# A fused RWKV-and-MoE layer: two value products in fp32r terms, and another order of the weight halves

## The chip, the cores and the metric

The kernel runs on one NeuronCore of a Trainium2 chip. The metric is device time in microseconds of one launch, as the median of several runs, lower is better. The engines named here: TensorE (PE, matrix products), VectorE (DVE), ScalarE (ACT, activation functions), GpSimd (POOL), SyncE (SP, which issues all DMA). Each engine runs its own list of instructions in order; semaphores hold one engine for another.

## The reference

Two layers over x of shape (8, 512, 512): batch, token, feature. The first is an RWKV time mix, the second a mixture of eight small experts with the top two chosen. Each has a residual and a layer norm behind it. Cut to what matters:

```python
shifted = jnp.pad(hidden, ((0, 0), (1, 0), (0, 0)))[:, :-1]
key   = hidden * time_mix_key   + shifted * (1.0 - time_mix_key)
value = hidden * time_mix_value + shifted * (1.0 - time_mix_value)
rec   = hidden * time_mix_receptance + shifted * (1.0 - time_mix_receptance)
k = key @ Wk
v = value @ Wv
r = jax.nn.sigmoid(rec @ Wr)
rwkv = _wkv(time_decay, time_first, k, v)   # a scan over the tokens: num, den, running max
x = _layernorm(x + (r * rwkv) @ Wo)
...
logits = x @ router_w.T ; gate = softmax(logits) * top2_mask
x = _layernorm(x + expert_mixture(x, gate))
```

## The kernel before

The features lie on the partitions. A **unit** is one batch and one block of 128 output features, so 8 batches of 4 units make 32 units, and the main loop runs over 32 **slots**, one unit each. All engines walk the same slots. A unit takes three products, key (PK), value (PV) and receptance (PR), each 128x512 out of four chunks of 128 input features; PE makes key(s+1), rec(s) and value(s+1) in slot s, and around them the projection of a token tile of the batch before (PP), its transposition (PT) and the expert layer (PH, PU).

The products are exact enough only if a plain fp32 operand is used, or if both operands are split. In the split form a value is written as high + low in the fp32r type (ACT copies the high half, POOL or DVE subtracts to get the low half), and each chunk gets three products: high by high, high of the input by low of the weight, low of the input by high of the weight. **Batch 0 uses the plain form** (`whole`, L316, weights as they were loaded into X1T, XN[0], XN[1]), **batches 1 to 7 the split form** (`split`, L330, L331, L336). The weight halves WKH, WKL, WVH, WVL, WRH, WRL are made during slots 0 to 6 while batch 0 is computed.

The order is written out by hand, engine by engine. What matters around the change:

- DVE in slot s: scan DEN (L871), times value (L878), scan NUM (L888), value now (L883), NU, the numerator (L895); then `scan_max` (L858) and `lead` (L864) of unit s+1, `gate` (L900) of unit s, `weigh` (L912, writes RW, the unit's result), and between them the mixes (L925) that make the inputs of the next batch: `mixes(b, which, chunks)`, with which 0 for key, 1 for value, 2 for receptance. In slot 1 DVE makes three key mixes of batch 1, then WKL's second half (L1048), then RW.
- ACT in slot s: two operations on PR (`receptance`), three Relu on PK (`decay_gates`), two more on PR (`log_g`, `factor`: without them `weigh` can't start), three Exp (`decay_exps`: without them the DEN scan can't start). All are recorded at L592. The high halves stand between them: WKH and WVH whole ahead of slot 0, WRH whole at the end of slot 0.
- POOL in slot s: DQ (L1213), wanted by `gate`; in slot 0 the four differences D of batch 1 (L1173), wanted by its mixes; in slot 1 the four blocks of WVL (L1244); then the low halves of batch 1's inputs (L1181).
- PE waits in `value(u)` for NU of unit u-1 (semaphore c), in `rec(u)` for RW of unit u-1 (rw), in `key(u)` for NUM of unit u-2 (num), and in batch 1's first unit for each high and low half of its input.

Of the kernel before, what the change touches and what calls it, by code (L numbers as in the profile page):

```python
# [29 lines left out]
def rwkv_moe_postln(nc, x, xt, vec, wk, wv, wr, wo, dr, up, tri, out):  # L30
    with ExitStack() as ctx:
# [169 lines left out]
        def sems(names):  # L201
            return {n: sem("s_" + n) for n in names.split()}

        q = sems("vec ws00 ws01 ws02 ws10 ws11 ws12 ws20 ws21 ws22 wo dr up tri out0 out1 out2 out3 xt0 xt1 xt2 xt3 xn0 xn1 xn2 xn3 xm0 xm1 xm2 xm3 "
# [104 lines left out]
        def _(eng):  # L309
            def whole(dst, stage, u, which):  # L310
                o = slice(128 * u, 128 * u + 128)
                eng.wait_ge(q[f"ws{which}{min(u, 2)}"], 16)
                for c in range(C):
                    if u == 0:
                        eng.wait_ge(q["kt"], C * which + c + 1)
                    last = eng.matmul(dst[:, :], stage[:, c, o], full(0, which, c), start=(c == 0), stop=(c == C - 1))  # L316
                return last

            def split(dst, weights, high, low, u, which, freed):
                b, j = divmod(u, C)  # L320
                o = slice(128 * j, 128 * j + 128)
                wh, wl = weights
                first = j == 0
                if b == 1:
                    eng.wait_ge(q["hw"], which + 1)
                    eng.wait_ge(q[("lwk", "lwv", "lwr")[which]], j + 1 if which else 2)
                for c in range(C):
                    if first:
                        eng.wait_ge(q["hi"], C * (3 * (b - 1) + which) + c + 1)
                    eng.matmul(dst[:, :], wh[:, c, o], high[:, c, :], start=(c == 0), stop=False)  # L330
                    eng.matmul(dst[:, :], wl[:, c, o], high[:, c, :], start=False, stop=False)  # L331
                    if first and C * (3 * (b - 1) + which) + c + 1 == ODD:
                        eng.wait_ge(q["rl1"], 1)
                    elif first:
                        eng.wait_ge(q["lo"], by_pool(C * (3 * (b - 1) + which) + c + 1))
                    last = eng.matmul(dst[:, :], wh[:, c, o], low[:, c, :], start=False, stop=(c == C - 1))  # L336
                    if j == C - 1 and c < C - 1:
                        last.then_inc(q[freed], 1)
                return last

            def key(u):
# [2 lines left out]
                last = split(PK[u % 2], (WKH, WKL), KH, KL, u, 0, "kc") if u >= C else whole(PK[u % 2], X1T, u, 0)  # L344
                last.then_inc(q["k"], 1)

            def value(u):
                eng.wait_ge(q["c"], u)
                last = split(PV, (WVH, WVL), VH, VL, u, 1, "vc") if u >= C else whole(PV, XN[0], u, 1)
                last.then_inc(q["v"], 1)  # L350

            def rec(u):
# [235 lines left out]
        def _(eng):  # L588
# [40 lines left out]
            def highs(b, which, chunks=range(C)):  # L629
                high, done, freed = ((KH, "k", "kc"), (VH, "v", "vc"), (RH, "r", "rc"))[which]  # L630
                for c in chunks:
                    eng.wait_ge(q["kt"], C * (3 * b + which) + c + 1)
                    if b > 1 and c < C - 1:
                        eng.wait_ge(q[freed], (C - 1) * (b - 2) + c + 1)
                    elif b > 1:
                        eng.wait_ge(q[done], C * b)
                    act("hi", high[:, c, :], full(b, which, c), ACT.Copy)
# [88 lines left out]
            eng.wait_ge(q["vec"], 16)  # L726
            act("etd", NTD, VEC[:, 0, :], ACT.Exp)

            def high_weights(i):
                stage, high = ((X1T, WKH), (XN[0], WVH), (XN[1], WRH))[i]  # L730
                for n in range(3):
                    eng.wait_ge(q[f"ws{i}{n}"], 16)
                act("hw", high[:, :, :], stage[:, :, :], ACT.Copy)

            decay_gates(0)
            decay_exps(0)
            high_weights(0)
            high_weights(1)
            for s in SLOTS:
                b, j = divmod(s, C)  # L740
                t2, t3 = NT * (b - 2), NT * (b - 3)
# [43 lines left out]
                if s < U - 1:  # L785
                    decay_exps(s + 1)
                if s == 0:
                    high_weights(2)
                if j == 3 and b and batch(b + 1):
                    highs(b + 1, 2, range(C - 1, C))  # L790
                for t in now[:1] if j == 3 and b < LAST else []:
# [61 lines left out]
        def _(eng):  # L853
# [190 lines left out]
                eng.tensor_tensor(D[:, c, :], XT[:, c, 1:T + 1], XT[:, c, 0:T], ALU.subtract).then_inc(q["d0"], 1)  # L1044

            def low_weights(lo):
                eng.wait_ge(q["hw"], 1)
                eng.tensor_tensor(WKL[:, lo:lo + 2, :], X1T[:, lo:lo + 2, :], WKH[:, lo:lo + 2, :].bitcast(F32),  # L1048
                                  ALU.subtract).then_inc(q["lwk"], 1)

# [9 lines left out]
            for s in SLOTS:  # L1060
                b, j = divmod(s, C)
                t2, t3 = NT * (b - 2), NT * (b - 3)
                now, past = tiles_of(s), tiles_of(s - 1)
                k = gated(s)
                scan_den(s)
                value_kept(s)
                if s == C:
                    eng.wait_ge(q["hi"], ODD)
                    eng.tensor_tensor(RL[:, C - 1, :], full(1, 2, C - 1), RH[:, C - 1, :].bitcast(F32), ALU.subtract)\
                       .then_inc(q["rl1"], 1)  # L1070
                scan_num(s)
                value_now(s)
                numerator(s)
                for t in past[1:]:
                    residual(t)
                if j == 0 and batch(b - 3):
                    residual2(t3 + 3)
                if j == 3 and s < U - 1 and batch(b - 2):
                    residual2(t2 + 1)
                if j == 1 and b:  # L1080
                    mixes(b + 1, 0, 3)
                if j == 3 and b:
                    mixes(b + 1, 2, 0)
                if j == 2 and s < U - 2 and batch(b - 2):
                    gated_low(b - 2)
                if C - 1 <= s < C * LAST:
                    gate(s)
                if s < U - 1:
                    scan_max(s + 1)
                    lead(s + 1)  # L1090
                if k is not None and s < U - 1:
                    gate_top(k)
                if s == 2:
                    mixes(1, 0, 3)
                if j == 3 and b:
                    mixes(b + 1, 2, 1)
                if not C - 1 <= s < C * LAST:
                    gate(s)
                if s == 1:
                    mixes(1, 0, 0, 1, 2)  # L1100
                if j == 2:
                    mixes(b + 1, 1, *(() if b else (0, 1)))
                if j == 3:
                    mixes(b + 1, 2, *((2, 3) if b else (0,)))
                if s == U - 1:
                    gate_scores(LAST - 1)
                if s < 2:
                    low_weights(2 * s)
                if s == C + 1:
                    eng.wait_ge(q["woh"], 1)  # L1110
                    eng.tensor_tensor(WOL[:, 2:4, :], X1T[:, 2:4, :], WOH[:, 2:4, :].bitcast(F32), ALU.subtract)\
                       .then_inc(q["wol1"], 1)
                weigh(s)
                for t in now[:1]:
                    residual(t)
                if j == 0 and b:
                    mixes(b + 1, 0, 0, 1, 2)
                if j == 2:
                    mixes(b + 1, 1, *(range(C) if b else (2, 3)))
                    if s < U - 2 and batch(b - 2):  # L1120
                        residual2(t2)
                if j == 3:
                    if b == 0:
                        mixes(b + 1, 2, 1, 2, 3)
                    if s < U - 1 and batch(b - 2):
                        residual2(t2 + 2)
                if s < U - 2 and gated(s + 1) is not None:
                    gate_scores(gated(s + 1))
# [34 lines left out]
        def _(eng):  # L1163
# [73 lines left out]
            difference(0, 2)  # L1237

            def low_weights(i, *blocks):
                stage, high, low, done = ((XN[0], WVH, WVL, "lwv"), (XN[1], WRH, WRL, "lwr"))[i - 1]  # L1240
                eng.wait_ge(q["hw"], i + 1)
                for j in blocks:
                    o = slice(128 * j, 128 * j + 128)
                    eng.tensor_tensor(low[:, :, o], stage[:, :, o], high[:, :, o].bitcast(F32), ALU.subtract)\  # L1244
                       .then_inc(q[done], 1)

            for s in SLOTS:
# [12 lines left out]
                if s == C + 1:  # L1260
                    eng.wait_ge(q["woh"], 1)
                    eng.tensor_tensor(WOL[:, 0:2, :], X1T[:, 0:2, :], WOH[:, 0:2, :].bitcast(F32), ALU.subtract)\
                       .then_inc(q["wol"], 1)
                if j == 0 and batch(b + 1):
                    for c in range(C):
                        difference(b + 1, c)
                if s == 1:
                    low_weights(1, *range(C))
                if j == 0 and batch(b - 3):
                    normalise2(t3 + 2)  # L1270
                if j == 2 and batch(b + 1):
# [82 lines left out]
```

## Time and profile before

| | us |
|---|---|
| median of 3 runs | 460.04 |
| lowest, highest | 459.71, 460.34 |
| the profiled execution | 459.98 |
| its span on the core | 458.2 |
| PE, busy in the span | 444.6 |
| DVE | 404.1 |
| ACT | 356.0 |
| POOL | 312.0 |

The span is what the trace covers; the time has 1.8 us more around it. Busy time is a sum over the whole span and says little of the first 66 us, in which the change lies: there the share of PE is lower and its waits have releasers, which the rows further down show. The granted TensorE clock stands at its full level in all of the forty slices but the last.

### The profile page before, as it was taken

To read this page: it belongs to the slowest core of one execution; us is meant where nothing else is said; L and a number is where in the kernel's file an instruction comes from. 1 tells how busy PE (TensorE), PEld (TensorE's weight loads), DVE (VectorE), ACT (ScalarE), POOL (GpSimd) and SP (SyncE) were. 2 spreads that over 40 slices of the span, in tenths; PEclk is the share of its full clock that TensorE was granted. 3 is DMA by queue.
4 is the path that set the end of the run, shared out by engine and by line. 5 is a ranking of instruction groups with operands and counts; after the bars stand their busy time and mean duration, and the time that the engine had idled before them with its cause. 6 is when DMAs were issued, how large, how long until landed. Compare 5 with 4: busy or idle time off the path is not lost.

```text
span 458.2 us, 6679 instructions
## 1 busy us (share of the span) xinstructions
PE 444.6 (97%) x1984; PEld 340.2 (74%) x1984; DVE 404.1 (88%) x616; ACT 356.0 (78%) x801; POOL 312.0 (68%) x300
## 2 busy tenths in 40 slices
PE   8999999999999999999999999999999999999993
PEld 3444567777888888888888888888888888888761
DVE  5989989899788989999898998989898996876976
ACT  1666757877888779888788888888798887768695
POOL 2355677588658998579858797569966694744334
PEclk9999999999999999999999999999999999999998
DMA  8703230033000042002320042100520022300016
GB/s 239 223 0 117 93 92 1 1 115 93 1 1 0 2 160 92 24 0 74 135 70 0 1 139 93 46 0 24 162 93 1 1 69 94 137 1 0 0 49 229
DMA packets 20244, 30.64 MB, mean 67 GB/s; under 512 B 2032, under 2 KB 7152, under 8 KB 20208
## 3 DMA queue, kind: packets, MB, share of 16 engines
q1 hardware_dynamic: 20208, 30.21, 20.3%
q8 instruction: 16, 0.26, 0.2%
q14 instruction: 20, 0.16, 0.1%
HBM read 21.82 MB, written 8.39 MB: 66 GB/s over the span
## 4 chain that ended last, share of the span: by engine, by line
PE 78%; DVE 5%; ACT 2%; POOL 2%; issue 1%; ACTq 0%; DVEq 0%
PE PH L449 5%; PE PV L330 5%; PE PV L336 5%; PE PV L331 5%; PE PR L336 5%; PE PR L330 5%; PE PK L330 5%; PE PR L331 5%; PE PK L336 5%; PE PK L331 5%; PE PP L359 4%; PE PP L360 4%; PE PP L364 4%; PE PT L431 3%; PE PP L379 2%
## 5 line engine op out<-in xcount | busy, mean ns | idle before, releaser
L592 ACT ACTIVATE PR<-PR 128x512 f32<-128x512 f32 x128 | 74.6, 583 | 29.8 <-PE PR L336 10.6
L1213 POOL TENSOR_TENSOR DQ<-DEN,EX 128x512 f32<-128x512 f32 x32 | 41.3, 1290 | 20.6 <-DVE DEN L871 20.6
L1219 POOL TENSOR_SCALAR NM<-SUM,RS 128x1 f32<-128x1 f32 x30 | 8.0, 267 | 62.1 <-ACT RS L592 62.1
L330 PE MATMUL PK<-KH,WKH 128*128 128x512 f32 x112 | 46.2, 413 | 0.6 <-DVE NUM L888 0.6
L925 DVE SCALAR_TENSOR_TENSOR KT<-D,VEC,XT 128x512 f32<-128x512 f32 x57 | 45.8, 851 | 0.0
L330 PE MATMUL PV<-VH,WVH 128*128 128x512 f32 x112 | 45.6, 407 | 0.0
L336 PE MATMUL PR<-RL,WRH 128*128 128x512 f32 x112 | 44.0, 393 | 0.7 <-POOL RL L1181 0.7
L330 PE MATMUL PR<-RH,WRH 128*128 128x512 f32 x112 | 44.5, 398 | 0.2 <-DVE RW L912 0.2
L336 PE MATMUL PV<-VL,WVH 128*128 128x512 f32 x112 | 43.9, 392 | 0.0
L336 PE MATMUL PK<-KL,WKH 128*128 128x512 f32 x112 | 43.9, 392 | 0.0
L331 PE MATMUL PK<-KH,WKL 128*128 128x512 f32 x112 | 43.8, 391 | 0.0
L331 PE MATMUL PV<-VH,WVL 128*128 128x512 f32 x112 | 43.8, 391 | 0.0
L331 PE MATMUL PR<-RH,WRL 128*128 128x512 f32 x112 | 43.7, 390 | 0.0
L1181 POOL TENSOR_TENSOR RL<-D,RH 128x512 fp32r<-128x512 f32 x27 | 39.5, 1490 | 4.6 <-ACT RH L592 4.6
L592 ACT ACTIVATE EX<-PK 128x512 f32<-128x512 f32 x32 | 19.1, 598 | 28.2 <-DVE PK L864 28.2
L871 DVE TENSOR_TENSOR_SCAN DEN<-PK,EX 128x512 f32<-128x512 f32 x32 | 38.9, 1216 | 2.3 <-ACT PK L592 1.6
L592 ACT ACTIVATE EX<-EX 128x512 f32<-128x512 f32 (+1 forms) x66 | 40.4, 612 | 0.1
L888 DVE TENSOR_TENSOR_SCAN NUM<-PK,EX 128x512 f32<-128x512 f32 x32 | 39.2, 1224 | 1.1
L1181 POOL TENSOR_TENSOR VL<-KT,VH 128x512 fp32r<-128x512 f32 x28 | 38.3, 1389 | 1.8 <-ACT VH L592 1.8
L858 DVE TENSOR_TENSOR_SCAN M<-CST,PK 128x512 f32<-128x512 f32 x32 | 38.7, 1210 | 0.1
L592 ACT ACTIVATE PK<-PK 128x512 f32<-128x512 f32 x64 | 38.4, 600 | 0.0
L1181 POOL TENSOR_TENSOR KL<-KT,KH 128x512 fp32r<-128x512 f32 x28 | 35.4, 1296 | 2.6 <-ACT KH L592 2.6
(275 smaller groups left out, 1285.7 us busy)
## 6 DMA issues: line engine op xcount, KB each, us to landing
XT<-in_xt SPq DMA_DIRECT2D x32, 256.0 KB, 3.3
XN<-in_x SPq DMA_DIRECT2D x28, 256.0 KB, 2.7
out<-XN SPq DMA_DIRECT2D x28, 256.0 KB, 2.0
X1T<-in_wo SPq DMA_DIRECT2D x1, 1024.0 KB, 5.1
XT<-in_x SPq DMA_DIRECT2D x4, 256.0 KB, 4.2
out<-XT SPq DMA_DIRECT2D x4, 256.0 KB, 2.4
X1T<-in_wk SPq DMA_DIRECT2D x2, 256.0 KB, 4.9
XN<-in_wv SPq DMA_DIRECT2D x2, 256.0 KB, 5.7
```

What stands on the lines that cost most here:

```text
L330: eng.matmul(dst[:, :], wh[:, c, o], high[:, c, :], start=(c == 0), stop=False)
L331: eng.matmul(dst[:, :], wl[:, c, o], high[:, c, :], start=False, stop=False)
L336: last = eng.matmul(dst[:, :], wh[:, c, o], low[:, c, :], start=False, stop=(c == C - 1))
L359: eng.matmul(projected_at(t), high(c), WOH[:, c, :], start=(c == 0), stop=False)
L449: last = eng.matmul(hidden_at(t), x1t_at(t)[:, c, :], DR[:, c, :], start=(c == 0), stop=(c == C - 1))
L592: eng.activation(*a, **k).then_inc(q[s], 1)
L858: eng.tensor_tensor_scan(M[:, 1:T + 1], TD[:, j:j + 1].to_broadcast([128, T]), PK[u % 2][:, :], NEG, ALU.add, ALU.max).then_inc(q["m"], 1)
L871: eng.tensor_tensor_scan(DEN[:, 1:T + 1], PK[u % 2][:, :], EX[:, 0, :], 0.0, ALU.mult, ALU.add)\
L888: eng.tensor_tensor_scan(NUM[:, 1:T + 1], PK[u % 2][:, :], EX[:, 0, :], 0.0, ALU.mult, ALU.add)\
L925: eng.scalar_tensor_tensor(out=full(b, which, c), in0=D[:, c, :], scalar=VEC[:, 2 + which, c:c + 1], in1=XT[:, c, 0:T], op0=ALU.mult, op1= ...
L1181: eng.tensor_tensor(lo[:, c, :], full(b, which, c), hi[:, c, :].bitcast(F32), ALU.subtract)\
L1213: eng.tensor_tensor(DQ[:, :], DEN[:, 0:T], EX[:, 1, :], ALU.add).then_inc(q["e"], 1)
```

## The change

It has four parts.

1. **Value products of units 2 and 3 of batch 0** are made by `value_by_halves`: twelve fp32r products in place of four plain ones. Their input halves are new: ACT copies the four chunks of batch 0's value input to VH (semaphore hi0) ahead of slot 0, POOL subtracts them into VL (lo0) in slot 0. VH is then taken again by batch 1, so its copies wait until four value products are done. POOL's low halves of the weight blocks 2 and 3 must be there as well.
2. **The weight halves come in pieces.** Ahead of slot 0 ACT makes the right half of WVH and the first two chunks of WKH; at the end of slot 0 the others; WRH moves from slot 0 to slot 1. The semaphore hw becomes hwk, hwv, hwr.
3. **POOL's list**: in slot 0 the VL subtractions and two WVL blocks, in slot 1 batch 1's differences and the other two WVL blocks.
4. **DVE's list**: in slot 1 the three key mixes of batch 1 move from ahead of WKL and RW to behind RW.

```diff
@@ -322,8 +322,8 @@
                 first = j == 0
                 if b == 1:
-                    eng.wait_ge(q["hw"], which + 1)
-                    eng.wait_ge(q[("lwk", "lwv", "lwr")[which]], j + 1 if which else 2)
+                    eng.wait_ge(q[("hwk", "hwv", "hwr")[which]], 2 if which < 2 else 1)
+                    eng.wait_ge(q[("lwk", "lwv", "lwr")[which]], (2, min(j + 3, C), j + 1)[which])
                 for c in range(C):
                     if first:
@@ -344,9 +344,26 @@
                 last.then_inc(q["k"], 1)
 
+            def value_by_halves(u):
+                o = slice(128 * u, 128 * u + 128)
+                eng.wait_ge(q["hwv"], 1)
+                eng.wait_ge(q["lwv"], u - 1)
+                for c in range(C):
+                    eng.wait_ge(q["hi0"], c + 1)
+                    eng.matmul(PV[:, :], WVH[:, c, o], VH[:, c, :], start=(c == 0), stop=False)
+                    eng.matmul(PV[:, :], WVL[:, c, o], VH[:, c, :], start=False, stop=False)
+                    eng.wait_ge(q["lo0"], c + 1)
+                    last = eng.matmul(PV[:, :], WVH[:, c, o], VL[:, c, :], start=False, stop=(c == C - 1))
+                return last
+
             def value(u):
                 eng.wait_ge(q["c"], u)
-                last = split(PV, (WVH, WVL), VH, VL, u, 1, "vc") if u >= C else whole(PV, XN[0], u, 1)
+                if u >= C:
+                    last = split(PV, (WVH, WVL), VH, VL, u, 1, "vc")
+                elif u >= C // 2:
+                    last = value_by_halves(u)
+                else:
+                    last = whole(PV, XN[0], u, 1)
                 last.then_inc(q["v"], 1)
 
@@ -630,6 +647,8 @@
                 for c in chunks:
                     eng.wait_ge(q["kt"], C * (3 * b + which) + c + 1)
+                    if b == 1 and which == 1:
+                        eng.wait_ge(q["v"], C)
                     if b > 1 and c < C - 1:
                         eng.wait_ge(q[freed], (C - 1) * (b - 2) + c + 1)
@@ -726,16 +745,29 @@
             act("etd", NTD, VEC[:, 0, :], ACT.Exp)
 
-            def high_weights(i):
-                stage, high = ((X1T, WKH), (XN[0], WVH), (XN[1], WRH))[i]
+            def loaded(i):
                 for n in range(3):
                     eng.wait_ge(q[f"ws{i}{n}"], 16)
-                act("hw", high[:, :, :], stage[:, :, :], ACT.Copy)
+
+            def key_weights(c):
+                loaded(0)
+                act("hwk", WKH[:, c:c + 2, :], X1T[:, c:c + 2, :], ACT.Copy)
+
+            def value_weights(o):
+                loaded(1)
+                act("hwv", WVH[:, :, o:o + H // 2], XN[0][:, :, o:o + H // 2], ACT.Copy)
+
+            def receptance_weights():
+                loaded(2)
+                act("hwr", WRH[:, :, :], XN[1][:, :, :], ACT.Copy)
 
             decay_gates(0)
             decay_exps(0)
-            high_weights(0)
-            high_weights(1)
+            for c in range(C):
+                eng.wait_ge(q["kt"], C + c + 1)
+                act("hi0", VH[:, c, :], full(0, 1, c), ACT.Copy)
+            value_weights(H // 2)
+            key_weights(0)
             for s in SLOTS:
                 b, j = divmod(s, C)
@@ -785,7 +817,10 @@
                     decay_exps(s + 1)
                 if s == 0:
-                    high_weights(2)
+                    key_weights(2)
+                    value_weights(0)
+                if s == 1:
+                    receptance_weights()
                 if j == 3 and b and batch(b + 1):
                     highs(b + 1, 2, range(C - 1, C))
@@ -1044,7 +1079,7 @@
 
             def low_weights(lo):
-                eng.wait_ge(q["hw"], 1)
+                eng.wait_ge(q["hwk"], lo // 2 + 1)
                 eng.tensor_tensor(WKL[:, lo:lo + 2, :], X1T[:, lo:lo + 2, :], WKH[:, lo:lo + 2, :].bitcast(F32),
                                   ALU.subtract).then_inc(q["lwk"], 1)
@@ -1096,8 +1131,6 @@
                 if not C - 1 <= s < C * LAST:
                     gate(s)
-                if s == 1:
-                    mixes(1, 0, 0, 1, 2)
                 if j == 2:
                     mixes(b + 1, 1, *(() if b else (0, 1)))
@@ -1111,6 +1144,8 @@
                        .then_inc(q["wol1"], 1)
                 weigh(s)
+                if s == 1:
+                    mixes(1, 0, 0, 1, 2)
                 for t in now[:1]:
                     residual(t)
@@ -1237,9 +1272,9 @@
 
             def low_weights(i, *blocks):
-                stage, high, low, done = ((XN[0], WVH, WVL, "lwv"), (XN[1], WRH, WRL, "lwr"))[i - 1]
-                eng.wait_ge(q["hw"], i + 1)
+                stage, high, low, made, done = ((XN[0], WVH, WVL, "hwv", "lwv"), (XN[1], WRH, WRL, "hwr", "lwr"))[i - 1]
                 for j in blocks:
+                    eng.wait_ge(q[made], 1 if i == 2 or j >= C // 2 else 2)
                     o = slice(128 * j, 128 * j + 128)
                     eng.tensor_tensor(low[:, :, o], stage[:, :, o], high[:, :, o].bitcast(F32), ALU.subtract)\
@@ -1261,11 +1296,17 @@
                     eng.tensor_tensor(WOL[:, 0:2, :], X1T[:, 0:2, :], WOH[:, 0:2, :].bitcast(F32), ALU.subtract)\
                        .then_inc(q["wol"], 1)
-                if j == 0 and batch(b + 1):
+                if s == 0:
+                    for c in range(C):
+                        eng.wait_ge(q["hi0"], c + 1)
+                        eng.tensor_tensor(VL[:, c, :], full(0, 1, c), VH[:, c, :].bitcast(F32), ALU.subtract)\
+                           .then_inc(q["lo0"], 1)
+                    low_weights(1, 2, 3)
+                if s == 1 or j == 0 and b and batch(b + 1):
                     for c in range(C):
                         difference(b + 1, c)
                 if s == 1:
-                    low_weights(1, *range(C))
+                    low_weights(1, 0, 1)
                 if j == 0 and batch(b - 3):
                     normalise2(t3 + 2)
```

VectorE in slot 1. PK, PR, KT, WKL, RW, DEN are lead of unit 2, gate of unit 1, batch 1's key mixes, low half of Wk, result of unit 1 and the first scan of unit 2. Before:

```order
L864 SCALAR_TENSOR_TENSOR PK<-PK,CST,M 128x512
L900 SCALAR_TENSOR_TENSOR PR<-PR,DQ 128x512
L925 SCALAR_TENSOR_TENSOR KT<-D,VEC,XT 128x512 x3
L1048 TENSOR_TENSOR WKL<-X1T,WKH 128x1024
L912 TENSOR_TENSOR RW<-NU,PR 128x512
L871 SCALAR_TENSOR_TENSOR DEN<-PK,EX 128x512
L878 TENSOR_TENSOR EX<-EX,PV 128x512
```

After, the same place:

```order
L899 SCALAR_TENSOR_TENSOR PK<-PK,CST,M 128x512
L935 SCALAR_TENSOR_TENSOR PR<-PR,DQ 128x512
L1083 TENSOR_TENSOR WKL<-X1T,WKH 128x1024
L947 TENSOR_TENSOR RW<-NU,PR 128x512
L960 SCALAR_TENSOR_TENSOR KT<-D,VEC,XT 128x512 x3
L906 SCALAR_TENSOR_TENSOR DEN<-PK,EX 128x512
L913 TENSOR_TENSOR EX<-EX,PV 128x512
```

The three mixes have gone from the place behind the gate to the place behind RW; the scan of unit 2 follows them at once.

GpSimd in slots 0 to 2, from the DQ of unit 0 on. D are the differences of batch 1, WVL the low halves of Wv. Before:

```order
L1213 TENSOR_TENSOR DQ<-DEN,EX 128x512
L1173 TENSOR_TENSOR D<-XT 128x512 x4
L1213 TENSOR_TENSOR DQ<-DEN,EX 128x512
L1244 TENSOR_TENSOR WVL<-XN,WVH 128x4x128 x4
L1213 TENSOR_TENSOR DQ<-DEN,EX 128x512
```

After, from the same DQ:

```order
L1248 TENSOR_TENSOR DQ<-DEN,EX 128x512
L1302 TENSOR_TENSOR VL<-RW,VH 128x512 x4
L1279 TENSOR_TENSOR WVL<-XN,WVH 128x4x128 x2
L1248 TENSOR_TENSOR DQ<-DEN,EX 128x512
L1208 TENSOR_TENSOR D<-XT 128x512 x4
L1279 TENSOR_TENSOR WVL<-XN,WVH 128x4x128 x2
```

Between the first two DQ there were four differences and are now six subtractions; between the second and the third there were four WVL blocks and are now four differences and two blocks.

## Rows read from the trace of the kernel before

**Rows 1.** Waits of TensorE (PE) from 67 to 420 us: us in total, times, longest

```profile
PE PR L330 <- DVE RW L912: 0.2, 1, 0.2
```

**Rows 2.** Waits of PE from 20 to 67 us

```profile
PE PV L316 <- DVE NU L895: 0.8, 2, 0.5
PE PR L336 <- POOL RL L1181: 0.7, 1, 0.7
PE PK L330 <- DVE NUM L888: 0.6, 1, 0.6
```

**Rows 3.** Timeline of PE: start, us, line, op, out<-in [idle before <-releaser]

```profile
32.36 3.70 PE L316 MATMUL PV<-RW,XN 128*128 128x512 f32 x8
35.90 1.02 PE L316 MATMUL PK<-RW,X1T 128*128 128x512 f32 x2
...
43.41 3.70 PE L316 MATMUL PV<-RW,XN 128*128 128x512 f32 x8 [0.49 <-DVE NU L895]
...
53.91 0.51 PE L330 MATMUL PK<-KH,WKH 128*128 128x512 f32 x1 [0.60 <-DVE NUM L888]
...
56.79 0.39 PE L330 MATMUL PV<-VH,WVH 128*128 128x512 f32 x1
```

**Rows 4.** Timeline of VectorE (DVE), slots 0 and 1

```profile
26.58 0.69 DVE L912 TENSOR_TENSOR RW<-NU,PR 128x512 f32<-128x512 f32 x1 [1.10 <-ACT PR L592]
27.66 1.23 DVE L871 TENSOR_TENSOR_SCAN DEN<-PK,EX 128x512 f32<-128x512 f32 x1 [0.39 <-ACT PK L592]
...
31.61 0.69 DVE L895 TENSOR_TENSOR NU<-NUM,PV 128x512 f32<-128x512 f32 x1
...
34.73 2.34 DVE L925 SCALAR_TENSOR_TENSOR KT<-D,VEC,XT 128x512 f32<-128x512 f32 x3
36.99 1.21 DVE L1048 TENSOR_TENSOR WKL<-X1T,WKH 128x1024 fp32r<-128x1024 f32 x1
38.13 0.67 DVE L912 TENSOR_TENSOR RW<-NU,PR 128x512 f32<-128x512 f32 x1
38.73 1.21 DVE L871 TENSOR_TENSOR_SCAN DEN<-PK,EX 128x512 f32<-128x512 f32 x1
```

**Rows 5.** Timeline of ScalarE (ACT), slots 0 and 1

```profile
16.47 1.90 ACT L592 ACTIVATE WKH<-X1T 128x2048 fp32r<-128x2048 f32 x1
...
21.60 1.20 ACT L592 ACTIVATE PR<-PR 128x512 f32<-128x512 f32 x2 [1.42 <-PE PR L316]
...
35.84 1.18 ACT L592 ACTIVATE PR<-PR 128x512 f32<-128x512 f32 x2
...
38.48 1.65 ACT L592 ACTIVATE KH<-KT 128x512 fp32r<-128x512 f32 x3
```

**Rows 6.** Timeline of GpSimd (POOL), slots 0 to 2

```profile
19.73 4.03 POOL L1173 TENSOR_TENSOR D<-XT 128x512 f32<-128x512 f32 x4
...
30.20 5.00 POOL L1244 TENSOR_TENSOR WVL<-XN,WVH 128x512 fp32r<-128x512 f32 x4
40.02 1.26 POOL L1213 TENSOR_TENSOR DQ<-DEN,EX 128x512 f32<-128x512 f32 x1 [4.82 <-DVE DEN L871]
```

**Rows 7.** Timelines of POOL and DVE, one POOL subtraction and mixes beside and without it

```profile
56.98 1.30 POOL L1244 TENSOR_TENSOR WRL<-XN,WRH 128x512 fp32r<-128x512 f32 x1
...
57.65 1.17 DVE L925 SCALAR_TENSOR_TENSOR D<-D,VEC,XT 128x512 f32<-128x512 f32 x1
...
59.35 2.07 DVE L925 SCALAR_TENSOR_TENSOR D<-D,VEC,XT 128x512 f32<-128x512 f32 x3
...
105.57 3.05 DVE L925 SCALAR_TENSOR_TENSOR D<-D,VEC,XT 128x512 f32<-128x512 f32 x3
```

**Rows 8.** Timelines of DVE and ACT, the end of slot 2

```profile
44.52 0.76 DVE L864 SCALAR_TENSOR_TENSOR PK<-PK,CST,M 128x512 f32<-128x512 f32 x1
...
45.31 0.60 ACT L592 ACTIVATE EX<-PK 128x512 f32<-128x512 f32 x1 [1.16 <-DVE PK L864]
...
48.65 0.69 DVE L912 TENSOR_TENSOR RW<-NU,PR 128x512 f32<-128x512 f32 x1 [0.80 <-ACT PR L592]
```

2 rows, old and new, of the table q are left out of this document.

## The prediction

> **What bounds the kernel now.** I read the waits of TensorE (PE) first, by stretch. From 67 us to 420 us PE waits once, 0.2 us [rows 1]: its work is gapless there, so whatever moves PE's position at 67 us moves the end by as much, and nothing behind it can give that back. All that can be won or lost by this change is therefore what it does to PE's position at 67 us. Between 20 and 67 us PE waits in three ways [rows 2]: for NU (the numerator of the unit before, by VectorE) twice, 0.8 us; for NUM once, 0.6 us; for RL (low half of the receptance operand, by GpSimd) once, 0.7 us.
>
> The timeline of PE gives the places [rows 3]. The value product of unit 3 starts at 43.41 after 0.49 us of waiting for NU of unit 2; the key product of unit 5 starts at 53.91 after 0.60 us of waiting for NUM of unit 3. The value product of unit 2 starts at 32.36, and NU of unit 1 had begun at 31.61 with 0.69 us to go [rows 4], so it starts the moment VectorE (DVE) lets it. DVE in the same stretch [rows 4] has hardly an idle moment: 1.10 us before RW of unit 0, 0.39 us before the DEN scan behind it, and then nothing up to 48.65. **So until 54 us the pace is DVE's, and PE follows.** The two chains that enter slot 4, NUM of unit 3 and RL, both start from DVE.
>
> **What the change takes from PE.** A value product in plain fp32 takes from 32.36 to 35.90, 3.54 us; twelve fp32r products take from 53.91 to 56.79, 2.88 us [rows 3]. That is 0.66 us less per unit, 1.32 us for units 2 and 3. Neither is on the path. Unit 2 now ends near 35.2 and unit 3's key product may start there; the receptance product of unit 2 then wants RW of unit 1, and value 3 stands behind the same NU of unit 2 as before. I book 0 for it. If DVE's pace were not the limit, it would be worth 1.32 us.
>
> **What it gives ACT.** Four 128x512 copies (hi0) stand ahead of the weight halves. Three such copies take 1.65 us from 38.48 [rows 5], so four take 2.2. The weight halves become one half of WVH and one of WKH, with 1.90 us for a whole [rows 5] 0.95 us each. 16.47 + 2.2 + 1.9 = 20.6 us, and the next work of ACT waits for PE until 21.60 [rows 5]: hidden by 1.0 us. In slot 0 the other two halves stand where the whole WRH stood (one whole matrix both ways, 0). WRH moves behind the exponentials of slot 1, at 38.48; the KH copies start at 40.4 instead of 38.48 and end at 42.0. The low halves of them wait on GpSimd behind DQ of unit 2 anyway, which starts at 40.02 now, 40.9 after the shift below, and ends 1.3 later. Hidden: 0. The added wait of the batch 1 value highs for four value products holds ACT at about 51 us for something finished at about 47: 0.
>
> **What it gives GpSimd (POOL).** Before, four differences take 4.03 us from 19.73, and four WVL pieces 5.00 us from 30.20 [rows 6], 1.25 us a piece. After, slot 0 has four low halves of the operand and two WVL pieces, 6 x 1.25 = 7.5 us: 19.73 to 27.2, free before DQ of unit 1, which takes about 1.25 us and ends where the pieces begin now, at 30.20. Slot 1 has four differences (30.2 to 34.2) and two WVL pieces (to 36.7). The differences are wanted by the three batch 1 key mixes, which start after 37 us: not late.
>
> **What it does to DVE.** This is the term that counts. Slot 1 now, behind the gate [rows 4]: three mixes 34.73 to 36.99, WKL 36.99 to 38.13, RW of unit 1 38.13, DEN of unit 2 at 38.73, no gap. RW waits for ACT's second PR operation; the two take 1.18 us from 35.84 [rows 5], to 37.02. Today the mixes and WKL lie over this wait. After the change only WKL does: it starts at 34.73 and needs 1.14 us (36.99 to 38.13), to 35.87, and DVE then waits to 37.05. RW takes 0.60 to 37.65, and only then come the three mixes. Three mixes with POOL quiet have 2.07 us in the row at 59.35 [rows 7], and as behind the three at 34.73 (2.34 in the row, 2.26 to the next start) 0.08 less to the next start, 1.99 us, so DEN of unit 2 starts at 39.64 instead of 38.73: **0.91 us late**. By the sum of gaps: 1.18 us of new idle, less 0.27 us that the mixes save since they no longer run beside a POOL operation (2.26 against 1.99).
>
> How far POOL disturbs this: the mix at 57.65 started beside a POOL subtraction (56.98, 1.30 us, so to 58.28) and took 1.17 us, where three alone take 2.07 or 0.69 each [rows 7]. In slot 0 the new POOL work may hold WKL until a POOL piece ends, at most 1.25 us. WKL has 1.10 us before RW of unit 0 must start, so RW is at worst 0.15 us late, and the DEN scan behind it waits 0.39 us for ACT until 27.66 [rows 4]: 0. In slot 1 WKL at 34.73 meets the first WVL piece (34.2 to 35.45): it ends near 36.6, still before 37.05; the second piece then ends at about 37.8 and catches the first mix for some 0.15 us, 0 to 0.2 more. Upper bound: all three mixes beside POOL, 3.05 us for three as at 105.57 [rows 7] instead of 1.99, which makes 0.91 + 1.06 = 1.97 us. I take 0.95 us, near the quiet value, since POOL's list is empty by 38 us.
>
> The Trainium skill says in "SBUF — State Buffer", section "Who interferes with whom", that a VectorE instruction with two SBUF inputs and a GpSimd instruction that reads SBUF share a read interface, and that the later one is blocked until the earlier ends. The row at 57.65 agrees (it gets going when the POOL piece ends at 58.28). By that rule the change would put WKL of slot 0 and of slot 1 behind one POOL piece each, both under cover; it adds at most the 0.2 us named above.
>
> **Does the delay reach PE?** From DEN of unit 2 on, everything is in DVE's order: NU of unit 2, max and lead of unit 3. ACT's exponents of unit 3 start at 45.31, when lead has ended (44.52 + 0.76) [rows 8], and the RW that waits for them, 48.65 with 0.80 us idle [rows 8], shifts too. So value 3 starts at 44.3, and with the shorter product ends near 47.2; the key product of unit 4 then stands for its last low half (0.9 late), receptance 3 for RW of unit 2 (50.25 instead of 49.34). NUM of unit 3 comes at 54.8: key 5 starts 0.9 late. RL comes down from gate, max, lead, exponents, RH: also 0.9 late. Both entries to slot 4 are late alike, so PE is at 67 us 0.95 us later than now, and the 1.32 us that it saved have become waiting: some 2 us before value 3 instead of 0.49, and about 1 us before key 5 instead of 0.60.
>
> **Sum.** Profiled execution 459.98 us (span 458.2 us), plus 0.95: 460.9; against the median of 460.04, which is the same to 0.06 us: 461.0 us.
>
> **Rivals.** (1) *PE was the pace*: then 1.32 us come out, 458.7 us. For it: PE waits only 1.4 us in 20 to 54 us. Against: each of these waits ends with DVE, and value 2 starts on NU to within 0.1 us. This is the side where the kernel gets faster; it decides itself at the start of value 3: if that is before 43.4 us, this rival is right, and it needs DVE not to be late. (2) *The shift is swallowed by the 0.80 us idle before RW of unit 2* [rows 8]: 0.91 - 0.80 leaves 0.1, 460.1 us. For it: DVE has that gap. Against: ACT, for which it waits, begins 0.03 us after lead, so the gap moves along. (3) *POOL beside the mixes*: up to 1.97 us, 462.0 us. It needs POOL's six new pieces to run 1 us later than I lay them. (4) *The change doesn't do what it says* in PE: the twelve products could cost as much as the eight passes; PE would not save, and the time is the same 461.0, since I book nothing for it.
>
> **Chances.** Forecast (0.85 to 1.3 us later) 0.70; swallowed 0.12; PE the pace 0.09; POOL beside the mixes 0.09. A measurement tells about 0.2%, 0.92 us, from no change, and my 0.95 is right on that line: of the 0.70 I give 0.38 to above and 0.32 to below. Slower 0.38 + 0.09 = 0.47; same 0.32 + 0.12 = 0.44; faster 0.09. The range reaches from the swallowed case to most of the third rival, 460.0 to 461.9 us; the 0.09 of the first and a bit of the third stay out.
>
> **What would show it.** Right: DVE idle of about 1.1 us before RW of unit 1, released by ACT; DEN of unit 2 at 39.5 to 39.9; PE waiting about 2 us for NU before value 3 (start 44.2 to 44.5) and over 1 us before key 5; the last RL wait unchanged near 0.7 us; PE gapless from 68 us. Wrong: value 3 at 43.4 or earlier, DVE without the new gap, or a stall of POOL past 28.9 us that makes DQ of unit 1, and with it the gate of unit 1, late.

## The result and the profile after

| | before | after |
|---|---|---|
| median (lowest to highest), us | 460.05 (459.69 to 460.34), 14 runs | 461.24 (460.75 to 461.67), 14 runs |
| the profiled execution, us | 459.98 | 461.66 |
| its span, us | 458.2 | 459.9 |

The ratio is 1.0025, 95% interval 1.0018 to 1.0032: slower by 1.19 us. The forecast was 461.0 us, in a range of 460.0 to 461.9 us.

The waits of PE from 20 to 68 us of the changed kernel (us in total, times, longest), beside [rows 2]:

```profile
PE PV L353 <- DVE NU L930: 2.1, 1, 2.1
PE PR L336 <- POOL RL L1216: 0.9, 2, 0.7
PE PV L316 <- DVE NU L930: 0.3, 1, 0.3
```

The two waits for NU were 0.8 us together and are 2.4 now; the wait for NUM before key 5 (0.6) is gone. The timeline of VectorE in slots 0 and 1, and RW of unit 2, answers to [rows 4] and [rows 8]:

```profile
24.58 1.49 DVE L1083 TENSOR_TENSOR WKL<-X1T,WKH 128x1024 fp32r<-128x1024 f32 x1
26.90 0.69 DVE L947 TENSOR_TENSOR RW<-NU,PR 128x512 f32<-128x512 f32 x1 [0.82 <-ACT PR L609]
27.97 1.23 DVE L906 TENSOR_TENSOR_SCAN DEN<-PK,EX 128x512 f32<-128x512 f32 x1 [0.39 <-ACT PK L609]
...
35.05 1.83 DVE L1083 TENSOR_TENSOR WKL<-X1T,WKH 128x1024 fp32r<-128x1024 f32 x1
37.36 0.69 DVE L947 TENSOR_TENSOR RW<-NU,PR 128x512 f32<-128x512 f32 x1 [0.48 <-ACT PR L609]
37.97 2.07 DVE L960 SCALAR_TENSOR_TENSOR KT<-D,VEC,XT 128x512 f32<-128x512 f32 x3
39.96 1.22 DVE L906 TENSOR_TENSOR_SCAN DEN<-PK,EX 128x512 f32<-128x512 f32 x1
...
49.89 0.69 DVE L947 TENSOR_TENSOR RW<-NU,PR 128x512 f32<-128x512 f32 x1 [0.80 <-ACT PR L609]
```

This execution as a whole begins 0.31 us later than that of before (DEN of unit 1 at 27.97 against 27.66; the first scan of the running max, at 11.30 before, is at 11.61). Executions differ in that: in the profiles of the runs below the first scan stands at 11.11 to 11.65, and two kernels with the same work up to there can lie 0.3 us and more apart. So distances are to be read, not positions: **from DEN of unit 1 to DEN of unit 2 it is 11.99 us, and was 11.07: 0.92 us more**, where the prediction had 0.91.

One thing is there that the prediction did not have. The timeline of PE at value 3:

```profile
44.65 0.50 PE L353 MATMUL PV<-VH,WVH 128*128 128x512 f32 x1 [2.08 <-DVE NU L930]
44.99 0.56 PE L354 MATMUL PV<-VH,WVL 128*128 128x512 f32 x1
45.34 0.63 PE L356 MATMUL PV<-VL,WVH 128*128 128x512 f32 x1
...
48.33 0.46 PE L353 MATMUL PV<-VH,WVH 128*128 128x512 f32 x1
...
49.10 0.40 PE L330 MATMUL PK<-KH,WKH 128*128 128x512 f32 x1
```

and the two windows of the same trace (busy us by engine, then the granted clock, DMA share, GB/s):

```profile
44.99:48.33 3.34, 3.34 (x9) 2.58 (x8) 3.31 (x5) 1.77 (x4) 1.22 (x1) 0.51 0.04 14
49.10:51.80 2.70, 2.70 (x13) 2.22 (x12) 1.91 (x3) 2.67 (x6) 1.15 (x1) 1.00 0.51 158
```

After 2.08 us of waiting the granted clock is at 0.51 for 3.34 us, the lower level of 1.2 GHz, and a product follows the one before after 0.35 to 0.43 us instead of 0.23. Value 3 takes 4.45 us (44.65 to 49.10) instead of 2.9. Receptance 3 starts later for it, and VectorE's gate of unit 3 now waits for it. The gate on VectorE:

```profile
56.83 0.70 DVE L935 SCALAR_TENSOR_TENSOR PR<-PR,DQ 128x512 f32<-128x512 f32 x1 [0.37 <-ACT PR L609]
```

and on PE the last product that waits in slot 4:

```profile
67.56 0.50 PE L336 MATMUL PR<-RL,WRH 128*128 128x512 f32 x1 [0.70 <-POOL RL L1216]
```

That product stood at 65.86 before and stands at 67.56: 1.70 us, which are 0.31 of the later beginning, 0.92 of VectorE's slot 1, and a rest of 0.47, which I put down to the slow clock: the gate of unit 3 stands 1.06 us behind NU of unit 3 instead of 0.61, and that accounts for 0.45 of it. The spans differ by the same 1.7 us (458.2 to 459.9); behind 68 us PE has the same waits in both traces.

The fourteen runs speak for that last part not being in all of them. Six, the profiled one among them, have a mean granted clock of 0.990 to 0.992 and take 461.33 to 461.67 us. The other eight have 0.994 to 0.997; six of them take 460.75 to 460.99, the last two 461.14 and 461.56. A stretch of 3.34 us at 0.51 lowers the mean over the span by 0.004, about the distance between the groups (0.991 and 0.996). Where the clock fell in the five low runs without a profile is not on record.

### The profile page after: what moved, and what is told of

It is laid out like the page before. It is cut to its first block, busy times and chain, and to the rows that moved or that the text cites. A ratio compares the mean times of both kernels' runs of the same rounds, so it can differ in the third digit from the quotient of the medians.

```text
span 459.9 us, 6713 instructions
## 1 busy us (share of the span) xinstructions
PE 445.8 (97%) x1992; PEld 343.8 (75%) x1992; DVE 404.9 (88%) x616; ACT 358.3 (78%) x807; POOL 318.8 (69%) x304
## 4 chain that ended last, share of the span: by engine, by line
PE 80%; DVE 5%; ACT 2%; issue 2%; POOL 2%; ACTq 0%; DVEq 0%
PE PH L466 5%; PE PV L330 5%; PE PK L330 5%; PE PV L336 5%; PE PK L336 5%; PE PK L331 5%; PE PV L331 5%; PE PR L336 5%; PE PR L330 5%; PE PR L331 5%; PE PP L377 4%; PE PP L376 4%; PE PP L381 4%; PE PT L448 3%; PE PP L396 2%
```

## The experiments

The theory: until 54 us VectorE sets the pace, and its slot 1 is 0.92 us longer. First, which part of the change makes it so, and is it that at all? Four kernels ran beside each other, with a kernel before of 460.05 us.

### The mixes ahead again

```diff
 # the changed kernel, VectorE
+                if s == 1:
+                    mixes(1, 0, 0, 1, 2)
                 if j == 2:
                     mixes(b + 1, 1, *(() if b else (0, 1)))
...
                 weigh(s)
-                if s == 1:
-                    mixes(1, 0, 0, 1, 2)
```

> The changed kernel with one part undone: the three key mixes of batch 1 stand ahead of WKL and RW of unit 1 again. Theory (the loss is VectorE's new gap before RW of unit 1): the gap goes, but the mixes and WKL now stand beside two WVL pieces of GpSimd (34.5 to 38), so they take 0.3 to 0.9 us longer than in the kernel before; DEN of unit 2 starts 0 to 0.7 us later than in the kernel before, the time is 460.0 to 460.7 us. Rival (the halves on ScalarE and GpSimd or the shorter products themselves cost the time): 461.2 us as in the changed kernel.

Measured: 461.34 us (461.27 to 461.82, 6 runs), ratio 1.0031 (1.0019 to 1.0042). Not recovered at all; the expectation missed, and the time is the one that the rival gave. Whether the rival's cause is right the time can't tell; the traces can. VectorE's timeline of this kernel, GpSimd's, and PE where it waits in slots 1 and 2:

```profile
34.64 3.65 DVE L960 SCALAR_TENSOR_TENSOR KT<-D,VEC,XT 128x512 f32<-128x512 f32 x3
38.21 1.21 DVE L1083 TENSOR_TENSOR WKL<-X1T,WKH 128x1024 fp32r<-128x1024 f32 x1
39.34 0.68 DVE L947 TENSOR_TENSOR RW<-NU,PR 128x512 f32<-128x512 f32 x1
39.94 1.21 DVE L906 TENSOR_TENSOR_SCAN DEN<-PK,EX 128x512 f32<-128x512 f32 x1
```

```profile
30.09 4.04 POOL L1208 TENSOR_TENSOR D<-XT 128x512 f32<-128x512 f32 x4
34.09 2.99 POOL L1279 TENSOR_TENSOR WVL<-XN,WVH 128x512 fp32r<-128x512 f32 x2
```

```profile
40.07 1.13 PE L316 MATMUL PR<-AGT,XN 128*128 128x512 f32 x2 [1.35 <-DVE RW L947]
...
44.63 0.50 PE L353 MATMUL PV<-VH,WVH 128*128 128x512 f32 x1 [0.85 <-DVE NU L930]
```

There is no gap before RW any more, and yet DEN comes later, 12.38 us behind the DEN of unit 1 (27.56). The three mixes meet both WVL pieces, each of which holds one mix up, and take 3.65 us instead of 2.34 [rows 4]. With the mixes ahead and GpSimd's new list the distance is 1.31 us longer than before; with the mixes behind RW, 0.92. So under GpSimd's new list the place behind RW is the cheaper of the two. PE's wait is here in two parts, 1.35 us for RW and 0.85 for NU, with work between them, and none of the six runs has a mean clock below 0.994. The prediction had the right sum for the kernel as it stands, but read alone it would have sent one to undo part 4, which is wrong.

### The mixes behind, alone

```diff
 # the kernel before, VectorE
-                if s == 1:
-                    mixes(1, 0, 0, 1, 2)
                 if j == 2:
...
                 weigh(s)
+                if s == 1:
+                    mixes(1, 0, 0, 1, 2)
```

> The kernel before with this part alone: the three key mixes of batch 1 behind RW of unit 1. Theory: DEN of unit 2 starts 0.9 us late, value 3 starts after about 1.4 us of waiting for NU, the clock of TensorE stays at its upper level, and the time is 460.9 to 461.1 us. Rival (the order alone is harmless): 460.05 us.

Measured: 461.15 us (460.80 to 461.41, 11 runs), ratio 1.0021 (1.0012 to 1.0030). The two DEN scans on VectorE:

```profile
28.02 1.23 DVE L871 TENSOR_TENSOR_SCAN DEN<-PK,EX 128x512 f32<-128x512 f32 x1 [0.39 <-ACT PK L592]
...
40.01 1.21 DVE L871 TENSOR_TENSOR_SCAN DEN<-PK,EX 128x512 f32<-128x512 f32 x1
```

They lie 11.99 us apart, as in the changed kernel. PE waits 1.4 us for NU before value 3:

```profile
44.70 3.70 PE L316 MATMUL PV<-RW,XN 128*128 128x512 f32 x8 [1.41 <-DVE NU L895]
```

None of the runs has a mean clock below 0.994. This part alone gives the whole of VectorE's 0.92 us, without halves, pieces or short products. GpSimd has its old list here; so with the mixes behind RW the new list adds nothing to the 0.92, and with them ahead it costs 1.31.

### Extra products in the wait before value 3

```diff
 # the changed kernel, TensorE
+                if s == 2:
+                    for _ in range(2):
+                        eng.matmul(PP[:, :], XN[0][:, 0, 0:128], RW[:, 3, :], start=True, stop=True)
                 if s < U - 1:
                     value(s + 1)
```

> The changed kernel with two extra fp32 products (about 1.7 us, result unused) ahead of value 3, in TensorE's wait for NU. Theory (the upper group of the changed kernel's times, 461.3 to 461.7 us, comes from the granted clock that falls to 1.2 GHz after the 2.1 us of waiting): all runs in the lower group, 460.7 to 461.0 us, granted clock 0.997 in the mean, value 3 takes 2.75 us instead of 4.45. Rival (the groups come from the loading of the first inputs or something else): two groups as before, median 461.2 us.

Measured: 460.97 us median (460.85 to 462.20, 9 runs), ratio 1.0021 (1.0011 to 1.0030). Seven of the nine lie at 460.85 to 461.15, one at 461.22, one at 462.20, none has a clock below 0.994. The profiled run:

```profile
42.32 1.88 PE L558 MATMUL PP<-RW,XN 128*128 128x512 f32 x4
44.56 0.51 PE L353 MATMUL PV<-VH,WVH 128*128 128x512 f32 x1 [0.37 <-DVE NU L933]
44.91 0.40 PE L354 MATMUL PV<-VH,WVL 128*128 128x512 f32 x1
45.14 0.40 PE L356 MATMUL PV<-VL,WVH 128*128 128x512 f32 x1
...
47.45 0.39 PE L330 MATMUL PK<-KH,WKH 128*128 128x512 f32 x1
...
55.06 0.50 PE L330 MATMUL PK<-KH,WKH 128*128 128x512 f32 x1 [0.81 <-DVE NUM L926]
```

Value 3 takes 2.89 us (44.56 to 47.45). PE does 1.7 us more work and the median lies 0.27 us below the changed kernel's: the low-clock runs are gone, none in nine against six in fourteen. So the group at 0.990 to 0.992 belongs to the idle time before value 3. Four of the nine times lie above the 460.7 to 461.0 us that were expected; the clock does not account for these.

### Plain value products

```diff
 # the changed kernel, TensorE
-                elif u >= C // 2:
-                    last = value_by_halves(u)
```

> The changed kernel with plain fp32 value products of units 2 and 3 again on TensorE (the halves are still made by ScalarE and GpSimd). Theory: TensorE was not the pace, so its 1.3 us come back without a loss: value 3 waits 1.4 us instead of 2.1, the clock stays at the upper level, 460.7 to 461.0 us, not slower than the changed kernel. Rival (the shorter products do win something in the changed kernel): 461.2 + 0.7 to 1.3 = 461.9 to 462.5 us.

Measured: 460.99 us (460.87 to 461.37, 11 runs), ratio 1.0022 (1.0013 to 1.0031), clock 0.994 to 0.997. Units 2 and 3 cost PE 1.3 us more and the kernel is not slower; by the medians it is 0.25 us faster than the changed one. PE waits 1.4 us before value 3 instead of 2.1:

```profile
44.45 3.70 PE L316 MATMUL PV<-RW,XN 128*128 128x512 f32 x8 [1.42 <-DVE NU L928]
```

The shorter products are worth nothing here, and by making the wait longer they bring in the slow clock.

### GpSimd's last WVL blocks held back

```diff
 # the changed kernel with the mixes ahead (as above), GpSimd
                 if s == 1:
+                    eng.wait_ge(q["lwk"], 2)
                     low_weights(1, 0, 1)
```

> The changed kernel with the three key mixes ahead of WKL and RW of unit 1 again, and with GpSimd's last two WVL blocks held until VectorE has made WKL. Theory, reformed after e1 (there the mixes took 3.65 us beside WVL pieces; GpSimd's later list is what costs VectorE the time, in whichever order it stands): the mixes take 2.0 us, DEN of unit 2 comes 10.8 us after DEN of unit 1 (before 11.07, changed 11.99, e1 12.38), and the time is 459.7 to 460.1 us. Rival (ScalarE's added work or the shorter products cost something by themselves): 460.5 us or more although DEN is on time.

Measured: 459.96 us (459.63 to 460.64, 11 runs) beside a kernel before of 460.16, ratio 0.9994 (0.9985 to 1.0003).

```profile
34.67 2.07 DVE L960 SCALAR_TENSOR_TENSOR KT<-D,VEC,XT 128x512 f32<-128x512 f32 x3
36.65 1.22 DVE L1083 TENSOR_TENSOR WKL<-X1T,WKH 128x1024 fp32r<-128x1024 f32 x1
37.79 0.68 DVE L947 TENSOR_TENSOR RW<-NU,PR 128x512 f32<-128x512 f32 x1
38.39 1.22 DVE L906 TENSOR_TENSOR_SCAN DEN<-PK,EX 128x512 f32<-128x512 f32 x1
```

DEN follows DEN of unit 1 (27.59) after 10.80 us, where 10.8 was expected. The same three mixes, at the same place of VectorE's list, took 3.65 us beside two WVL pieces, 2.34 beside the end of one and 2.07 with none. The whole loss of the changed kernel is gone, with ScalarE's added copies and the short products still in. So ScalarE's part costs nothing, the short products nothing but the clock, and what is left is VectorE and GpSimd at one place in slot 1.

### Half of WKL on GpSimd, in the kernel before

```diff
 # the kernel before
 # VectorE
-                if s < 2:
+                if s < 1:
                     low_weights(2 * s)
 # GpSimd, slot 0, behind the differences
+                if s == 0:
+                    eng.wait_ge(q["lwk"], 1)
+                    eng.tensor_tensor(WKL[:, 2:4, :], X1T[:, 2:4, :], WKH[:, 2:4, :].bitcast(F32),
+                                      ALU.subtract).then_inc(q["lwk"], 1)
```

> The kernel before with one move: the second half of WKL (1.14 us of VectorE in slot 1) is made by GpSimd in slot 0, behind the first half and before DQ of unit 1. Theory (until 54 us VectorE sets the pace): RW of unit 1 starts at 37.05, when ScalarE lets it, DEN of unit 2 at 37.65 instead of 38.73, and the whole is 1.1 us faster, 458.8 to 459.2 us. Rival (TensorE, full to 97%, sets the pace as much): no more than the 0.49 us that value 3 waits, 459.5 us or more.

Measured: 459.43 us (459.19 to 460.61, 11 runs) beside 460.16, ratio 0.9986 (0.9978 to 0.9995): 0.73 us faster by the medians. That is less than the 1.1 expected and more than the 0.49 of the rival, though the interval (0.2 to 1.0 us) has room for the rival too; the trace decides. The timeline of VectorE:

```profile
34.54 2.33 DVE L925 SCALAR_TENSOR_TENSOR KT<-D,VEC,XT 128x512 f32<-128x512 f32 x3
36.86 0.69 DVE L912 TENSOR_TENSOR RW<-NU,PR 128x512 f32<-128x512 f32 x1
37.94 1.22 DVE L871 TENSOR_TENSOR_SCAN DEN<-PK,EX 128x512 f32<-128x512 f32 x1 [0.39 <-ACT PK L592]
```

RW starts when it should, but DEN then waits 0.39 us for ScalarE's exponents of unit 2. DEN to DEN is 10.47 us (from 27.47) instead of 11.07. The next limit lies 0.60 us below the first. The last product of PE that waits for RL comes at 65.08 instead of 65.86; without the 0.19 us by which this execution begins earlier (first scan at 11.11 against 11.30) that is 0.59, more than the rival's 0.49.

### A mix in the gap of slot 2, on top of that

```diff
 # the kernel of the last experiment, VectorE
-                    mixes(b + 1, 1, *(() if b else (0, 1)))
+                    mixes(b + 1, 1, *(() if b else (0, 1, 2)))
...
                 weigh(s)
...
-                    mixes(b + 1, 1, *(range(C) if b else (2, 3)))
+                    mixes(b + 1, 1, *(range(C) if b else (3,)))
```

> The kernel of e5 with one more move: in slot 2 the third value mix of batch 1 (0.66 us) stands ahead of RW of unit 2, in the 0.80 us in which VectorE waits there for ScalarE, and no longer behind it. Theory (e5 showed ScalarE's exponents as the next limit of a DEN scan: it gained 0.6 us there instead of 1.1): the move takes 0.66 us off VectorE, but DEN of unit 3 can't start before ScalarE's exponents of unit 3 end, 0.3 to 0.4 us ahead of where the scan starts now; so 0.3 to 0.4 us come out, 459.0 to 459.2 us by a kernel before of 460.1. Rival (VectorE alone sets the pace): 0.66 us come out, 458.8 us or less.

> The kernel of e5 again, beside e7 on the same chip, for the difference between the two: 459.4 us, 0.6 to 0.8 us under the kernel before.

Measured: 459.77 us (459.26 to 460.09) and, for the kernel of the last experiment again, 459.31 (459.17 to 459.89), 11 runs each, beside a kernel before of 460.10; ratios 0.9991 (0.9982 to 1.0000) and 0.9985 (0.9976 to 0.9993). The repeat confirms the gain. The further move does not win 0.3 to 0.4 us and not 0.66; both theories missed. VectorE and then GpSimd in slot 2:

```profile
46.12 3.10 DVE L925 SCALAR_TENSOR_TENSOR KT<-D,VEC,XT 128x512 f32<-128x512 f32 x3
49.15 0.68 DVE L912 TENSOR_TENSOR RW<-NU,PR 128x512 f32<-128x512 f32 x1
```

```profile
47.27 1.41 POOL L1181 TENSOR_TENSOR KL<-KT,KH 128x512 fp32r<-128x512 f32 x1 [2.64 <-ACT KH L592]
```

The third mix would begin at 47.44, when the last KL subtraction has begun (47.27 to 48.68), and it ends behind it. RW comes 10.77 us behind DEN of unit 2 (38.38 to 49.15) instead of 9.93 (37.94 to 47.87), and with one mix less behind RW, DEN of unit 3 comes 12.03 us behind DEN of unit 2 instead of 11.86: 0.17 us lost. The medians lie 0.46 us apart, the fastest runs 0.09; the trace explains 0.17 of it, and the rest is of the size of the scatter of the beginnings. The 0.80 us in which VectorE stood idle were not free: GpSimd was reading SBUF in them.

## Why the prediction was right, point by point

- **The pace.** That VectorE sets it up to 54 us was shown from both sides: 0.92 us added there come out as 1.10 us by the medians and 0.91 by the fastest runs (the order alone, 461.15 and 460.80 against 460.05 and 459.89), 0.60 us taken away as 0.73 to 0.79, and 1.3 us put back on PE as nothing. The first rival (PE sets the pace) is out with that. The second (swallowed by the 0.80 us before RW of unit 2) is out by the trace: RW of unit 2, at 49.89 in the changed kernel, still has its 0.80 us behind ScalarE. The third (GpSimd beside the mixes) did not come, since the mixes had no piece beside them; the kernel with the mixes ahead shows it at work. The fourth is out by the 2.87 us below.
- **VectorE's slot 1.** Forecast 0.91 by the quiet rows, 0.95 with a little disturbance; measured 0.92. The prediction doesn't agree with itself on what lies inside. Its sum has 1.18 us of new idle time, and its sign has about 1.1; its paragraph on GpSimd has WKL end near 36.6 behind a WVL piece, which leaves 0.45. That came: WKL took 1.83 us and ended at 36.88 (36.57 without the 0.31 of the later beginning), and the idle time is 0.48. So that sign was wrong. The total does not depend on it, because RW starts when ScalarE's second PR operation lets it, however much of the wait WKL fills. The mixes took 2.07 us, as quiet as assumed: 0.04 us too much was booked.
- **What the Trainium skill says of the shared read side** ("SBUF — State Buffer", section "Who interferes with whom": a VectorE instruction with two SBUF inputs contends with a GpSimd instruction that reads SBUF) was used as a remark of 0.2 us and holds the whole second half of the story: it is why the mixes could not stay ahead, and why the idle 0.80 us of slot 2 could not be filled. The traces agree: WKL is recorded with 1.83 us behind a piece and 1.21 without one, three mixes with 3.65 beside two pieces and 2.07 beside none.
- **GpSimd.** Its list in slot 0 was laid at 7.5 us and took 8.4 (20.05 to 28.48), since WKL in turn holds one piece for about 1.0 us. 0.80 us were left before DQ of unit 1, as the timeline of the changed kernel shows:

```profile
20.05 4.95 POOL L1302 TENSOR_TENSOR VL<-RW,VH 128x512 fp32r<-128x512 f32 x4
24.95 3.53 POOL L1279 TENSOR_TENSOR WVL<-XN,WVH 128x512 fp32r<-128x512 f32 x2
29.28 1.27 POOL L1248 TENSOR_TENSOR DQ<-DEN,EX 128x512 f32<-128x512 f32 x1 [0.80 <-DVE DEN L906]
```

- **ScalarE.** Its added work ahead of slot 0 is hidden, with 1.05 us left where 1.0 was forecast:

```profile
21.91 1.20 ACT L609 ACTIVATE PR<-PR 128x512 f32<-128x512 f32 x2 [1.05 <-PE PR L316]
```

- **PE.** Twelve products take 2.87 us for value 2 (32.67 to 35.54), forecast 2.88; wait before value 3 2.08 us, forecast some 2. Missed: that this wait lets the clock fall in some of the runs. The wait before key 5 was forecast as about 1 us (over 1 us among the signs). It is 0 in the profiled execution, because value 3 is longer there, and 0.81 us with the extra products; that sign was wrong too. The clock is the term that was left out: 0.47 us in the profiled execution and about 0.25 us in the median (461.24 against 460.97 and 460.99 of the two kernels that lack it). With it the 461.0 of the forecast becomes the 461.24 measured.
- **The chances.** The case forecast at 0.70 came. For slower or same the prediction drew a line at 0.2%, 0.92 us, with its own 0.95 on it. The median is 1.19 us above that of before, but the interval of the ratio (1.0018 to 1.0032) has the line in it; the two kernels without the low-clock runs lie at 0.92 and 0.94 us, and the one with the order alone at 1.10. On which side of that line the change falls is therefore hardly more than luck, and 0.38 against 0.32 said as much.

What stays open: what sets the beginning of an execution, which scatters by up to 0.54 us in the profiles (the first scan at 11.11 to 11.65) and blurs differences of that size between medians; and the one run of 462.20 us with the extra products, of which there is no profile. The 1.31 us of GpSimd's new list with the mixes ahead come from one profiled execution; the 0.92 us of the order stand in four, those of the changed kernel, of the order alone, of the extra products and of the plain value products. Why a wait of 2.08 us let the clock fall in six runs and left it up in eight is open.

## What to carry to other kernels

Before an engine's instructions are moved into or out of an idle stretch, lay the other engine's list beside it: here an instruction of VectorE with two SBUF inputs (the mixes, WKL) cost its own time only where GpSimd read nothing from SBUF beside it, and the profile shows the lost time as a longer instruction, not as a wait. Work taken off TensorE, which follows VectorE here, was worth nothing, and less than nothing where its longer wait was followed by a fall of its clock. Of a stretch that is bound by VectorE, take work off VectorE, and look at what is late next: here 0.60 of 1.14 us came out before ScalarE's exponents were the limit.

## What the runs showed of the hardware

- After 2.08 us in which TensorE waited, the granted clock stood at the lower level (1.2 GHz) for 3.34 us in the profile of the changed kernel. Six of its fourteen runs have a low mean clock (0.990 to 0.992). None has among 22 runs of the two kernels that wait 1.4 us there, nine with extra products in the wait, and six of the kernel that waits 1.35 and 0.85 us with work between (all 0.994 to 0.997).
- WKL, a VectorE subtraction of 128x1024 with both inputs in SBUF, was recorded with 1.21 us alone (slot 1 of the kernel before), 1.49 and 1.83 us beside GpSimd subtractions (slots 0 and 1 of the changed kernel). GpSimd's piece is held up in turn: two WVL pieces took 3.53 us there and 2.55 in the kernel that holds them back.
- Three mixes of 128x512, both tensor inputs in SBUF, were recorded with 2.07 us alone, 2.34 beside the end of one GpSimd piece and 3.65 beside two.
